# A four-layer graph network on one core: earlier rank prefix, eight term buffers, places in two pieces, and edge-row scatters moved between other work

## The chip, the cores and the metric

The kernel runs on 1 core of one Trainium2 chip, as one launch. The metric is device microseconds of one execution; lower is better. The time before is the median of 3 runs.

## The reference, cut to what matters

Four graph layers over 3125 nodes (256 features) and 50,000 edges sorted by target, each added to a residual. The first, with attention, is the one that the change touches, together with the sum of edge attributes that the second layer needs:

```python
def gat_conv(h, src, dst, W, al, ar, residual):
    feat = (h @ W).reshape(N, H, D)
    el = jnp.sum(feat * al, axis=-1)
    er = jnp.sum(feat * ar, axis=-1)
    e = jax.nn.leaky_relu(el[src] + er[dst], 0.2)
    ex = jnp.exp(e - emax[dst])
    a = ex / denom[dst]
    rst = jax.ops.segment_sum(feat[src] * a[:, :, None], dst, num_segments=N)
    ...
# layer 0: gat_conv twice.  Layer 1:
sum3d = segment_sum(edge_attr @ W_sum + b_sum, src, num_segments=num_nodes)
cent_term = sigmoid(centralities @ W_cent + b_cent)
vor_term = sigmoid(voronoi_values @ W_vor + b_vor)
```

Layer 2 sums by relation, layer 3 has two convolutions with batch norm.

## The kernel before, in words

The program has three phases (two attention passes, a middle, a tail). All that changes lies in the first. Edges are 392 columns of 128; nodes are 25 tiles of 128. The engines run hand-written streams that meet at semaphores.

**Setup.** PE makes 25 encoder products (L1218) for the cent and vor terms, ACT takes their sigmoids into `sigb` (L1152, three buffers in turn; a buffer is free again once its sum is stored), POOL adds the two halves (L1133, "the sums") and SP stores the result to `term_d` (L1099). DVE meanwhile ranks half of the edges by source tile (`rank_half`): a table (L577), a running sum along it (L580), totals per tile (L585), then a wait for three small products of PE (`rank_prefix`, L616 to L618, issued on PE behind encoder tile 8), and from these the places `attr_pos` to which the 196 edge columns of this half go (L599 to L611, one increment of `s_pos`). After that DVE makes the id columns, the low bits (L1197, turned by PE behind the encoder), the first norm, the second half's ranks, masks and step tables.

**Scatter.** Edge attributes must be added up by source, though the edges are sorted by target. SP loads seven columns at a time into one of three buffers `abuf` (`stage_attr`, L529 and L531), and POOL scatters each column to its sorted place in `attr_d` (L568). A buffer is loaded again when its seven scatters have landed. A half of the edges is 28 groups, 196 columns.

**A pass.** PE, ACT and DVE look up the attention scores of all edges (L866 to L969, 98 groups, "the look"), DVE takes a softmax by scans (L987 to L1023), ACT raises it and sends it to HBM and back (L1060 to L1065). Then come 220 steps: POOL gathers the feature rows of an edge pair into a ring of 28 slots (L179, two indirect DMAs a pair, 392 a pass), ACT scales them (L241, L246) and counts the pair ready, PE multiplies by one-hot matrices (L374) and DVE adds (L299). Beside each step runs one over the sorted attribute rows of that half, which SP loads from `attr_d` (`load_sorted_attr`, L258). A slot is gathered anew when the steps that use it are done: pair 28 waits for the first step (L239 counts the slot free).

**The order on POOL** is written out: 25 sums, 196 scatters of the first half, 392 gathers of pass one, 196 scatters of the second half, 392 gathers of pass two. SP's order follows it: three groups staged at the start, then the term stores, the low bits, the other groups of the half, three groups of the second half, the sorted rows.

Of the kernel before, what the change touches and what calls it, by code (L numbers as in the profile page):

```python
# [6 lines left out]
ALU = mybir.AluOpType  # L7
ACT = mybir.ActivationFunctionType
AX = mybir.AxisListType
# [43 lines left out]
GROUP = 7  # L53
GROUPS = HC // GROUP
BUFS = 3
LOOKS = EC // 4
# [23 lines left out]
def gnn_program(nc, t, out):  # L80
# [92 lines left out]

    def gather_pairs(pool, g, table, index, ring):
        for u in range(PAIRS):
# [229 lines left out]
    def carve(area, at, shape, dt=F32):  # L405
# [67 lines left out]
    carry = carve(arena_flat[0:HEADS, :], ARING * AW, (3, P))  # L473
    sigb = carve(arena_flat, ARING * AW, (3, 2 * D))
    term_rows = term_d.rearrange("(n p) f -> n p f", p=P)
# [18 lines left out]
        sem(x) for x in ("enc_zeroed", "enc_load", "encoded", "sigmoids", "terms_added"))  # L494
    term_stored = [sem(f"term_stored{k}") for k in range(3)]
    s_back = [sem(f"terms_back{k}") for k in range(5)]
    staged = [sem(f"staged{k}") for k in range(BUFS)]
# [43 lines left out]
    def load_terms(sp, q):  # L541
        k = q - TERM_FROM
        if k == 0:
            sp.wait_ge(s_exw, 32)
            for b in range(3):
                sp.wait_ge(term_stored[b], 16 * len(range(b, NT, 3)))
        if 0 <= k < 5:
            sp.dma_start(term[:, 5 * k:5 * k + 5, :],
                         term_d.rearrange("(n p) f -> p n f", p=P)[:, 5 * k:5 * k + 5, :]).then_inc(s_back[k], 16)

    def sp_weights(sp, l, first):
        for g in range(first, GROUPS):
            stage_attr(sp, GROUPS * l + g)
        if l == 0:
            for g in range(BUFS):
                stage_attr(sp, GROUPS + g)
        sp.wait_ge(s_sum[l], LOOKS + 2)
        for k in range(BUFS):
            sp.wait_ge(scattered[k], 16 * GROUP * len(range(k, GROUPS * (l + 1), BUFS)))
        load_sorted_attr(sp, steps[l], l, aring, between=(lambda q: load_terms(sp, q)) if l else None)  # L560

    def pool_scatter(pool, l):
        pool.wait_ge(s_pos, l + 1)
        for g in range(GROUPS * l, GROUPS * (l + 1)):
            at = GROUP * g
            pool.wait_ge(staged[g % BUFS], 32 * (g // BUFS + 1))
            for k in range(GROUP):
                pool.indirect_dma_start(  # L568
                    out=attr_d, in_=abuf[:, g % BUFS, k, :], in_offset=None,
                    out_offset=bass.IndirectOffsetOnAxis(ap=attr_pos[:, at + k:at + k + 1], axis=0),  # L570
                ).then_inc(scattered[g % BUFS], 16)

    def rank_half(dve, h):
# [23 lines left out]
        dve.drain()  # L597
        for n in range(NT):
            dve.scalar_tensor_tensor(out=running[:, n, :], in0=running[:, n, :], scalar=offset[:, n:n + 1],  # L599
                                     in1=mk[:, n, :], op0=ALU.add, op1=ALU.mult)  # L600
        dve.drain()
        dve.reduce_sum(pos[:, :], running.rearrange("p n j -> p j n"), AX.X)
        dve.drain()
        dve.tensor_copy(pos_i[:, 0, :], pos[:, :])
        dve.drain()
        dve.tensor_scalar(pos_i[:, 1, :], pos_i[:, 0, :], 7, None, ALU.logical_shift_right)
        dve.drain()
        dve.tensor_scalar(pos_i[:, 0, :], pos_i[:, 0, :], P - 1, None, ALU.bitwise_and)
        dve.tensor_scalar(pos[:, :], pos_i[:, 1, :], float(h * HC * P), None, ALU.add)
        dve.drain()  # L610
        dve.scalar_tensor_tensor(out=attr_pos[:, at:at + HC], in0=pos_i[:, 0, :], scalar=float(HC),  # L611
                                 in1=pos[:, :], op0=ALU.mult, op1=ALU.add).then_inc(s_pos, 1)

# [119 lines left out]
    def spread_tables(pe):  # L733
        pe.wait_ge(s_sp, 1)
        pe.matmul(p_last[0:NT, 0:PAIRS], ones[0:1, 0:NT], last_f[0:1, :], start=True, stop=True).then_inc(s_sp, 1)
        pe.wait_ge(s_prefix, 2)
        pe.wait_ge(s_pos, 2)
        pe.matmul(p_rank[0:NT, 128:130], upto[0:NT, 0:NT], col_f[0:NT, :], start=True, stop=True)\
# [132 lines left out]
    def act_look(act, l):  # L871
# [34 lines left out]
    def dve_look(dve, l):  # L906
# [4 lines left out]
        if l == 0:  # L911
            for k in range(3):
                dve.wait_ge(term_stored[k], 16 * len(range(k, NT, 3)))
        dve.tensor_copy(tab[:, 0, :], flat)
# [154 lines left out]
    with nc.Block() as block:  # L1069
        @block.sync  # L1070
        def _(sp):
# [25 lines left out]
            for n in range(NT):  # L1097
                sp.wait_ge(s_term, n + 1)
                sp.dma_start(term_rows[n, :, :], sigb[:, n % 3, 0:D]).then_inc(term_stored[n % 3], 16)  # L1099
            for q in range(2):  # L1100
                for c in range(4):
                    sp.wait_ge(s_loc, 4 * q + c + 1)
                    sp.dma_start(lo_d[q, c * QC:(c + 1) * QC, :], loT[0:QC, 4 * q + c, :]).then_inc(s_low, 16)
            sp_weights(sp, 0, BUFS)
            sp.wait_ge(steps[0].step_done, T + NHOT)
            sp.wait_ge(steps[0].attr_done, T + NHOT)
            sp_weights(sp, 1, BUFS)
            for k in range(3):
                sp.wait_ge(kept[k], 16 * (9 if k == 0 else 8))
            for k in range(5):  # L1110
                sp.wait_ge(s_back[k], 16)

        @block.gpsimd
        def _(pool):
# [16 lines left out]
            for n in range(NT):  # L1131
                pool.wait_ge(s_sig, n + 1)
                pool.tensor_tensor(sigb[:, n % 3, 0:D], sigb[:, n % 3, 0:D], sigb[:, n % 3, D:2 * D], ALU.add)\  # L1133
                    .then_inc(s_term, 1)
            pool.wait_ge(s_ready, 2)
            pool_scatter(pool, 0)
# [11 lines left out]
        def _(act):  # L1148
            for n in range(NT):
                act.wait_ge(s_enc, n + 1)  # L1150
                wait_from(act, term_stored[n % 3], 16 * (n // 3))
                act.activation(sigb[:, n % 3, :], banks[n % 2][:, :], ACT.Sigmoid).then_inc(s_sig, 1)  # L1152
            act_first_project(act)
# [834 lines left out]
```

## Time and profile before

| | before |
|---|---|
| runs, median | 3409.36 us (3409.08, 3409.36, 3410.53) |
| profiled execution | one such execution; its span, first to last instruction, is 3410.2 us |
| POOL busy | 2412.8 us (71%) |
| PE busy | 2202.9 us (65%), mean granted clock 0.833 |
| DVE busy | 2099.5 us (62%) |
| ACT busy | 1368.3 us (40%) |
| DMA | 465.58 MB, 137 GB/s |

The profiled execution's own time is not listed apart from the three; its span lies between the lowest and the highest of them. Busy shares are means over stages: the first attention pass ends near 875 us, the second near 1638 us, the middle and tail fill the rest. Of POOL's DMA instructions the busy time is that of making the descriptors; the data move afterwards.

### The profile page before, as it was taken

The numbers are of one execution on the slowest core, as the hardware profiler recorded it, in microseconds if no ns is written. First come the engines' busy times: TensorE is split into PE (matmuls) and PEld (weight loads), VectorE is DVE, ScalarE is ACT, GpSimd is POOL, SyncE is SP. The second block draws the span as 40 slices with busy tenths as digits, with TensorE's granted clock in tenths as the row PEclk, the third lists the DMA queues.
The fourth block names the chain that finished last, engine by engine and source line by source line (L and its number), as shares of the span: only waits on it lengthen the run. The fifth ranks groups of instructions, "written<-read, shape, count | busy, mean of one in ns | idle before, by whom it ended". The sixth has DMA issues, their size and how long they took to land. (4 is left out here: it accounts for less than half of the span.)

```text
span 3410.2 us, 73948 instructions
## 1 busy us (share of the span) xinstructions
PE 2202.9 (65%) x11271; PEld 1571.4 (46%) x11272; DVE 2099.5 (62%) x5434; ACT 1368.3 (40%) x4627; POOL 2412.8 (71%) x2428
## 2 busy tenths in 40 slices
PE   5566367776665377766786666675666675666666
PEld 2355355555455265555434444453444444444443
DVE  7999877666499867766774444454444444444445
ACT  2366389998566399988670000020000013000004
POOL 5877767777777777777737777757777753777772
PEclk9789789988899789988797777787777887777787
DMA  4488734443688654443783333423333322333331
GB/s 141 120 215 229 223 101 137 137 126 104 183 230 225 198 152 145 138 121 105 208 277 110 109 109 109 125 91 107 108 108 108 109 72 87 108 109 107 109 107 55
DMA packets 347323, 465.58 MB, mean 137 GB/s; under 512 B 112217, under 2 KB 262972, under 8 KB 343812
## 3 DMA queue, kind: packets, MB, share of 16 engines
q0 software_dynamic: 111808, 284.19, 28.9%
q1 hardware_dynamic: 161972, 111.43, 11.3%
q10 hardware_dynamic: 73236, 67.28, 7.3%
q14 instruction: 288, 2.36, 0.2%
q8 instruction: 19, 0.31, 0.0%
HBM read 385.51 MB, written 76.97 MB: 136 GB/s over the span
## 5 line engine op out<-in xcount | busy, mean ns | idle before, releaser
L374 PE MATMUL t_ps<-t_ring,shared 128*128 x2640 | 920.8, 504 | 533.7 <-ACTq L218 439.8
L374 PEld LDWEIGHTS t_ps<-t_ring,shared 128*128 128x128 f32 x2640 | 611.6, 248 | 842.7 <-issue 748.2
L179 POOL DMA_INDIRECT ring<-feat_d,srcC x784 | 780.1, 995 | 253.4 <-issue 210.6
L179 POOL DMA_INDIRECT t_ring<-feat_d,srcC x756 | 725.5, 960 | 275.2 <-issue 216.6
L246 ACT ACTIVATE ring<-ring,exC 128x64 f32<-128x64 f32 x3136 | 788.2, 335 | 0.0
L374 PE MATMUL bank<-ring,arena 128*128 x1408 | 438.7, 438 | 166.6 <-ACT ring L246 129.7
L299 DVE TENSOR_TENSOR acc<-acc,t_ps 128x256 f32 x440 | 185.3, 421 | 519.6 <-PE t_ps L374 518.6
L568 POOL DMA_INDIRECT attr_d<-abuf,attr_pos x392 | 407.1, 1038 | 119.5 <-issue 119.5
L179 POOL DMA_INDIRECT t_ring<-rel_d,relC x378 | 358.6, 949 | 162.7 <-issue 106.5
L283 DVE TENSOR_SCALAR shared<-lane,dlocT,weightT 128x128 f32<-128x128 f32 x1320 | 410.0, 362 | 54.8 <-PE t_ps L374 27.5
L1747 ACT COPY t_ring<-t_pt 128x512 f32<-128x512 f32 (+1 forms) x8 | 4.2, 526 | 971.1 <-PE t_pt L1722 971.1
L374 PEld LDWEIGHTS bank<-ring,arena 128*128 128x128 f32 x1408 | 267.5, 211 | 240.0 <-issue 210.8
L969 PE MATMUL wide<-arena 128*128 128x100 bf16 x4704 | 260.5, 216 | 172.8 <-ACT arena L888 150.9
L969 PEld LDWEIGHTS wide<-arena 128*128 128x128 bf16 x4704 | 235.9, 103 | 197.8 <-DVE arena L930 106.2
L299 DVE TENSOR_TENSOR X<-X,t_ps 128x256 f32 x220 | 92.5, 420 | 251.0 <-PE t_ps L374 250.2
L299 DVE TENSOR_TENSOR acc<-acc,bank 128x261 f32 x352 | 150.3, 427 | 153.1 <-PE bank L374 146.0
L277 DVE TENSOR_TENSOR arena<-lane,dlocT 128x256 f32<-128x256 f32 x440 | 185.1, 421 | 66.9 <-issue 32.1
L884 ACT ACTIVATE arena<-arena,minus_part 128x512 bf16<-128x512 bf16 x196 | 141.4, 721 | 180.3 <-issue 114.2
L936 DVE TENSOR_TENSOR arena<-wide,shared 128x800 f32<-128x800 f32 x196 | 191.3, 976 | 8.6 <-PE wide L969 8.0
L1688 ACT ACT_TABLE_LOAD x1 | 1.3, 1283 | 485.5 <-DVE mv L1675 485.5
L945 DVE TENSOR_REDUCE shared<-arena 128x800 f32 (+1 forms) x196 | 190.4, 972 | 0.1
L364 PEld LDWEIGHTS bank<-arena 128*128 128x128 f32 x704 | 142.7, 206 | 71.8 <-issue 45.8
(307 smaller groups left out, 2615.9 us busy)
## 6 DMA issues: line engine op xcount, KB each, us to landing
arena<-lo_d ACTq DMA_DIRECT2D x392, 128.0 KB
t_ring<-feat_d SPq DMA_DIRECT2D x1664, 1.0 KB
t_ring<-feat_d ACTq DMA_DIRECT2D x1664, 1.0 KB
rel_d<-mid_stage SPq DMA_DIRECT2D x25, 1024.0 KB, 4.6
arena<-attr_d SPq DMA_DIRECT2D x98, 260.0 KB, 3.1
abuf<-in_attr SPq DMA_DIRECT2D x56, 448.0 KB
t_ring<-rel_d SPq DMA_DIRECT2D x832, 1.0 KB
t_ring<-rel_d ACTq DMA_DIRECT2D x832, 1.0 KB
```

The costliest lines, as they stand in the source:

```text
L179: pool.indirect_dma_start(out=ring[:, u % RING, j, 0:D], out_offset=None, in_=table, in_offset=bass.IndirectOffsetOnAxis(ap=index[:, u, j: ...
L246: last = act.activation(part_of_row, part_of_row, ACT.Copy, scale=exC[:, bass.ds(u, 1), j, h])
L277: last = dve.tensor_tensor(hot[:, k % NHOT, :, :], lane[:, :].unsqueeze(1).to_broadcast([P, 2, P]), dlocT[:, bass.ds(s, 1), :].rearrange(" ...
L283: last = dve.tensor_scalar(hot[:, k % NHOT, j, :], lane[:, :], dlocT[:, bass.ds(s, 1), j], weightT[:, bass.ds(s, 1), j], ALU.is_equal, ALU ...
L299: dve.tensor_tensor(acc[:, tile, 0:g.width], acc[:, tile, 0:g.width], ps[k % NHOT][:, 0:g.width], ALU.add).then_inc(g.added, 1)
L364: pe.matmul(ps_a[k % NHOT][:, 0:AW - 1], hot_a[:, k % NHOT, :], aring[:, slot, 0:AW - 1], start=True, stop=True).then_inc(g.attr_done, 1)
L374: last = pe.matmul(ps[k % NHOT][:, 0:g.width], hot[:, k % NHOT, j, :], ring[:, slot, j, 0:g.width], start=(j == 0), stop=(j == 1))
L568: pool.indirect_dma_start(out=attr_d, in_=abuf[:, g % BUFS, k, :], in_offset=None, out_offset=bass.IndirectOffsetOnAxis(ap=attr_pos[:, at ...
L884: act.activation(apart[:, k % 2, :], lo[:, k, 1, :], ACT.Abs, bias=minus_part[:, 0:1])\
L936: dve.tensor_tensor(cand[:, k % 2, :, :, :], pk[k % 2][:, :, :].rearrange("p b (s x) -> p (b s) x", x=P)[:, :, 0:HEADS * NT] .rearrange("p ...
L945: dve.tensor_reduce(e[:, bass.ds(4 * c, 4), :], cand[:, k % 2, :, :, :].rearrange("p (j q) h n -> p j h q n", q=2), AX.XY, ALU.add).then_i ...
L969: last = pe.matmul(pk[k % 2][:, j // 2, at:at + HEADS * NT], looked[:, k % 2, q, j * P:(j + 1) * P], tab[:, piece, q * HEADS * NT:(q + 1) ...
```

## The change

1. `rank_prefix(pe, 0)` stands behind encoder tile 3 instead of tile 8.
2. `sigb` has eight buffers instead of three, at another place of the arena; everything that uses that place later waits for the term stores.
3. The places of the first half come in two pieces, columns 0 to 27 and 28 to 195, each with its own increment of `s_pos`.
4. From sum 12 on, POOL issues one scatter behind each sum: 13 of the first half's 196 stand between and right behind the sums.
5. 35 of the second half's scatters (five groups) stand behind the first 28 pairs' gathers of pass one; the other 161 stay behind the last gather of that pass.
6. SP stages groups 3 and 4 ahead of the low bits, and of the second half five groups ahead of the sorted rows of pass one and three more between them. With three buffers, groups 31 and 32 wait for scatters of groups 28 and 29.

```diff
+FIRST = 4 * GROUP
+EARLY = 5
+SIGS = 8
+MEET = 12
...
-    sigb = carve(arena_flat, ARING * AW, (3, 2 * D))
+    sigb = carve(arena_flat, 4624, (SIGS, 2 * D))
...
+    def stage_later(sp, q):
+        if 12 <= q < 12 + BUFS:
+            stage_attr(sp, GROUPS + EARLY + q - 12)
...
         if l == 0:
-            for g in range(BUFS):
+            for g in range(EARLY):
                 stage_attr(sp, GROUPS + g)
         sp.wait_ge(s_sum[l], LOOKS + 2)
...
-        load_sorted_attr(sp, steps[l], l, aring, between=(lambda q: load_terms(sp, q)) if l else None)
+        load_sorted_attr(sp, steps[l], l, aring, between=(lambda q: (load_terms if l else stage_later)(sp, q)))
...
+    def scatter_column(pool, c):
+        g, k = c // GROUP, c % GROUP
+        if c == 0 or c == FIRST or c == HC:
+            pool.wait_ge(s_pos, 1 + (c >= FIRST) + (c >= HC))
+        if k == 0:
             pool.wait_ge(staged[g % BUFS], 32 * (g // BUFS + 1))
...
+        for r in (slice(0, FIRST), slice(FIRST, HC)) if h == 0 else (slice(0, HC),):
+            place_columns(dve, h, r)
+
+    def place_columns(dve, h, r):
+        w = r.stop - r.start
+        if w == FIRST:
+            dve.tensor_tensor(running[:, :, r], running[:, :, r],
+                              offset[:, :].unsqueeze(2).to_broadcast([P, NT, w]), ALU.add)
+            dve.drain()
+            dve.tensor_tensor(running[:, :, r], running[:, :, r], mk[:, :, r], ALU.mult)
+        else:
+            for n in range(NT):
+                dve.scalar_tensor_tensor(out=running[:, n, r], in0=running[:, n, r], scalar=offset[:, n:n + 1],
+                                         in1=mk[:, n, r], op0=ALU.add, op1=ALU.mult)
...
-        pe.wait_ge(s_pos, 2)
+        pe.wait_ge(s_pos, 3)
...
             act.wait_ge(s_low, 16 * 8)
+            for k in range(SIGS):
+                act.wait_ge(term_stored[k], TERM_STORES[k])
...
+            for g in range(BUFS, BUFS + 2):
+                stage_attr(sp, g)
             for q in range(2):
                 for c in range(4):
                     sp.wait_ge(s_loc, 4 * q + c + 1)
...
-            sp_weights(sp, 0, BUFS)
+            sp_weights(sp, 0, BUFS + 2)
...
-            sp_weights(sp, 1, BUFS)
+            sp_weights(sp, 1, EARLY + BUFS)
...
+                if n == MEET:
+                    pool.wait_ge(s_ready, 2)
+                if n >= MEET:
+                    scatter_column(pool, n - MEET)
+            for c in range(NT - MEET, HC):
+                scatter_column(pool, c)
...
-            gather_pairs(pool, steps[0], feat_d, srcC, ring)
-            pool_scatter(pool, 1)
+            gather_pairs(pool, steps[0], feat_d, srcC, ring, range(0, RING))
+            for c in range(HC, HC + EARLY * GROUP):
+                scatter_column(pool, c)
+            gather_pairs(pool, steps[0], feat_d, srcC, ring, range(RING, PAIRS))
+            for c in range(HC + EARLY * GROUP, 2 * HC):
+                scatter_column(pool, c)
...
-                wait_from(act, term_stored[n % 3], 16 * (n // 3))
+                wait_from(act, term_stored[n % SIGS], 16 * (n // SIGS))
...
-                if n == 8:
+                if n == 3:
                     pe.wait_ge(s_ready, 1)
                     rank_prefix(pe, 0)
```

POOL, from the sums to the end of pass one's gathers. L568 is a scatter, L179 a gather, L1133 a sum; in the changed kernel they are L577, L183 and L1157. Before:

```order
L1133 TENSOR_TENSOR arena<-arena 128x256 x25
L568 DMA attr_d<-abuf,attr_pos 50176x130 x196
L1140 MEMSET ring 128x56
L179 DMA ring<-feat_d,srcC 128x256 x392
L568 DMA attr_d<-abuf,attr_pos 50176x130 x196
```

The same stretch of the changed kernel, from the last of the alternating sums on:

```order
L1157 TENSOR_TENSOR arena<-arena 128x256
L577 DMA attr_d<-abuf,attr_pos 50176x130 x184
L1168 MEMSET ring 128x56
L183 DMA ring<-feat_d,srcC 128x256 x56
L577 DMA attr_d<-abuf,attr_pos 50176x130 x35
L183 DMA ring<-feat_d,srcC 128x256 x336
L577 DMA attr_d<-abuf,attr_pos 50176x130 x161
```

Twelve scatters stand singly between the last thirteen sums, and 35 have moved from behind all 392 gathers to behind the first 56.

SP, where pass one's sorted rows are loaded (L258 before, L262 now; L529 and L531, now L534 and L536, stage a group). Before:

```order
L529 DMA abuf<-in_attr 128x7x128
L531 DMA abuf<-src_f 128x7x1
L258 DMA arena<-attr_d 128x520 x49
L529 DMA abuf<-in_attr 128x7x128
```

And in the changed kernel:

```order
L534 DMA abuf<-in_attr 128x7x128
L536 DMA abuf<-src_f 128x7x1
L262 DMA arena<-attr_d 128x520 x13
L534 DMA abuf<-in_attr 128x7x128
L536 DMA abuf<-src_f 128x7x1
L262 DMA arena<-attr_d 128x520
```

Two more pairs of staging stand ahead of the first load of sorted rows, and three stand between the loads, from the thirteenth on.

## Rows read from the trace of the kernel before

**Rows 1.** The page: busy us, share of the span and instructions of each engine.
```profile
PE 2202.9 (65%) x11271; PEld 1571.4 (46%) x11272; DVE 2099.5 (62%) x5434; ACT 1368.3 (40%) x4627; POOL 2412.8 (71%) x2428
```
**Rows 2.** POOL's groups: count, busy us, mean ns, idle before. Stretch 71 to 345.6.
```profile
L568 POOL DMA_INDIRECT attr_d<-abuf,attr_pos x196 | 215.0, 1097 | 59.6 <-issue 59.6
```
**Rows 3.** The same, stretches 345.6 to 424, then 438 to 868.3.
```profile
L179 POOL DMA_INDIRECT ring<-feat_d,srcC x56 | 60.6, 1081 | 16.9 <-issue 16.8
L179 POOL DMA_INDIRECT ring<-feat_d,srcC x336 | 327.8, 976 | 117.1 <-issue 86.9 <-ACTq L239 30.2
```
**Rows 4.** The same, stretches 868.3 to 1120.1, then 1120.1 to 1199.25.
```profile
L568 POOL DMA_INDIRECT attr_d<-abuf,attr_pos x196 | 192.0, 980 | 59.8 <-issue 59.8
L179 POOL DMA_INDIRECT ring<-feat_d,srcC x56 | 62.1, 1108 | 17.1 <-issue 17.1
```
**Rows 5.** POOL's timeline: start, us, instruction [idle before]. Gathers 56 and 57, pass one.
```profile
422.20 0.95 POOL L179 DMA_INDIRECT ring<-feat_d,srcC  x1 [0.30 <-issue]
438.15 0.95 POOL L179 DMA_INDIRECT ring<-feat_d,srcC  x1 [14.99 <-ACTq L239]
```
**Rows 6.** POOL's timeline: gather 57 of pass two.
```profile
1199.30 0.95 POOL L179 DMA_INDIRECT ring<-feat_d,srcC  x1 [0.31 <-issue]
```
**Rows 7.** PE's timeline: the first step of pass one and of pass two.
```profile
435.73 2.10 PE L374 MATMUL bank<-ring,arena 128*128 x4 [1.47 <-ACT ring L246]
1192.32 2.10 PE L374 MATMUL bank<-ring,arena 128*128 x4 [1.49 <-ACT ring L246]
```
**Rows 8.** ACT's groups in 438 to 600, then one of its groups in 438 to 870.
```profile
L246 ACT ACTIVATE ring<-ring,exC 128x64 f32<-128x64 f32 x616 | 154.8, 335 | 0.0
L241 ACT COPY ring<-exC 128x8 f32 x192 | 35.8, 187 | 39.2 <-issue 16.8 <-DMA ring<-feat_d,srcC 16.8 <-PE bank L374 5.4
```
**Rows 9.** POOL's timeline where the sums end and the scatters begin.
```profile
70.13 0.72 POOL L1133 TENSOR_TENSOR arena<-arena 128x256 f32<-128x256 f32 x1 [0.79 <-ACT arena L1152]
71.03 1.20 POOL L568 DMA_INDIRECT attr_d<-abuf,attr_pos  x1 [0.17 <-issue]
...
87.80 0.96 POOL L568 DMA_INDIRECT attr_d<-abuf,attr_pos  x1 [0.30 <-issue]
89.06 5.52 POOL L568 DMA_INDIRECT attr_d<-abuf,attr_pos  x1 [0.31 <-issue]
94.89 10.07 POOL L568 DMA_INDIRECT attr_d<-abuf,attr_pos  x1 [0.30 <-issue]
```
**Rows 10.** DVE's timeline: totals, the wait for the prefix, the second half's running sum.
```profile
23.75 0.61 DVE L585 TENSOR_TENSOR offset<-total,ring 128x25 f32<-128x25 f32 x1
41.86 0.15 DVE L587 COPY col_f<-wide 25x1 f32<-25x1 f32 x1 [17.50 <-PE wide L618]
...
93.82 10.37 DVE L580 TENSOR_TENSOR_SCAN ring<-ones,ring 128x4900 f32<-128x4900 f32 x1
```
**Rows 11.** PE's timeline: prefix, and the last encoder products.
```profile
40.59 0.62 PE L616 MATMUL wide<-total,before 128*128 128x25 f32 x2
...
57.27 12.14 PE L1218 MATMUL bank<-shared 4*128 4x512 f32 x14
```
**Rows 12.** ACT's timeline: sigmoids of tiles 3 and 4, 9 and 10.
```profile
32.83 1.08 ACT L1152 ACTIVATE arena<-bank 128x512 f32<-128x512 f32 x2 [19.89 <-DMA term_d<-arena]
...
43.85 0.60 ACT L1152 ACTIVATE arena<-bank 128x512 f32<-128x512 f32 x1 [2.56 <-PE bank L1218]
45.56 0.60 ACT L1152 ACTIVATE arena<-bank 128x512 f32<-128x512 f32 x1 [1.11 <-PE bank L1218]
```
**Rows 13.** Busy us of PE, PEld, DVE, ACT, POOL in two stretches; PEclk, DMA share, GB/s.
```profile
16.00:33.00 17.00, 0.00 (x0) 0.00 (x0) 8.21 (x4) 0.17 (x1) 8.30 (x2) 1.00 0.99 293
33.00:41.00 8.00, 7.53 (x10) 2.83 (x11) 0.00 (x0) 3.00 (x6) 3.57 (x5) 1.00 0.19 66
```
**Rows 14.** SP's timeline: loads of sorted rows. Waits in 875 to 1192: total, times, longest.
```profile
387.75 27.46 SPq L258 DMA_DIRECT2D arena<-attr_d  x16
PE bank L1053 <- DMA acc<-weight_d: 17.2, 1, 17.2
```

More of the change, by code:

```diff
@@ L172, in __init__, with gather_pairs @@
                 self.landed.append(at.at)
-    def gather_pairs(pool, g, table, index, ring):
-        for u in range(PAIRS):
+    def gather_pairs(pool, g, table, index, ring, pairs=range(PAIRS)):
+        for u in pairs:
             if u >= RING:
@@ L494, in gnn_program @@
         sem(x) for x in ("enc_zeroed", "enc_load", "encoded", "sigmoids", "terms_added"))
-    term_stored = [sem(f"term_stored{k}") for k in range(3)]
-    s_back = [sem(f"terms_back{k}") for k in range(5)]
+    term_stored = [sem(f"term_stored{k}") for k in range(SIGS)]
+    s_back = term_stored[0:5]
+    TERM_STORES = [16 * len(range(k, NT, SIGS)) for k in range(SIGS)]
     staged = [sem(f"staged{k}") for k in range(BUFS)]
@@ L544, in load_terms @@
             sp.wait_ge(s_exw, 32)
-            for b in range(3):
-                sp.wait_ge(term_stored[b], 16 * len(range(b, NT, 3)))
+            for b in range(SIGS):
+                sp.wait_ge(term_stored[b], TERM_STORES[b])
         if 0 <= k < 5:
@@ L559, in sp_weights @@
             sp.wait_ge(scattered[k], 16 * GROUP * len(range(k, GROUPS * (l + 1), BUFS)))
-        load_sorted_attr(sp, steps[l], l, aring, between=(lambda q: load_terms(sp, q)) if l else None)
[L562 to L565, printed above, removed]
-            pool.wait_ge(staged[g % BUFS], 32 * (g // BUFS + 1))
[L567 to L571, printed above, removed]
+        load_sorted_attr(sp, steps[l], l, aring, between=(lambda q: (load_terms if l else stage_later)(sp, q)))
[4 more added lines that the diff above has]
+        if k == 0:
+            pool.wait_ge(staged[g % BUFS], 32 * (g // BUFS + 1))
+        pool.indirect_dma_start(
+            out=attr_d, in_=abuf[:, g % BUFS, k, :], in_offset=None,
+            out_offset=bass.IndirectOffsetOnAxis(ap=attr_pos[:, c:c + 1], axis=0),
+        ).then_inc(scattered[g % BUFS], 16)
     def rank_half(dve, h):
@@ L597, in rank_half @@
         dve.drain()
-        for n in range(NT):
-            dve.scalar_tensor_tensor(out=running[:, n, :], in0=running[:, n, :], scalar=offset[:, n:n + 1],
-                                     in1=mk[:, n, :], op0=ALU.add, op1=ALU.mult)
+        for r in (slice(0, FIRST), slice(FIRST, HC)) if h == 0 else (slice(0, HC),):
[11 more added lines that the diff above has]
+                                         in1=mk[:, n, r], op0=ALU.add, op1=ALU.mult)
         dve.drain()
-        dve.reduce_sum(pos[:, :], running.rearrange("p n j -> p j n"), AX.X)
+        dve.reduce_sum(pos[:, r], running[:, :, r].rearrange("p n j -> p j n"), AX.X)
         dve.drain()
-        dve.tensor_copy(pos_i[:, 0, :], pos[:, :])
+        dve.tensor_copy(pos_i[:, 0, r], pos[:, r])
         dve.drain()
-        dve.tensor_scalar(pos_i[:, 1, :], pos_i[:, 0, :], 7, None, ALU.logical_shift_right)
+        dve.tensor_scalar(pos_i[:, 1, r], pos_i[:, 0, r], 7, None, ALU.logical_shift_right)
         dve.drain()
-        dve.tensor_scalar(pos_i[:, 0, :], pos_i[:, 0, :], P - 1, None, ALU.bitwise_and)
-        dve.tensor_scalar(pos[:, :], pos_i[:, 1, :], float(h * HC * P), None, ALU.add)
+        dve.tensor_scalar(pos_i[:, 0, r], pos_i[:, 0, r], P - 1, None, ALU.bitwise_and)
+        dve.tensor_scalar(pos[:, r], pos_i[:, 1, r], float(h * HC * P), None, ALU.add)
         dve.drain()
-        dve.scalar_tensor_tensor(out=attr_pos[:, at:at + HC], in0=pos_i[:, 0, :], scalar=float(HC),
-                                 in1=pos[:, :], op0=ALU.mult, op1=ALU.add).then_inc(s_pos, 1)
+        dve.scalar_tensor_tensor(out=attr_pos[:, h * HC + r.start:h * HC + r.stop], in0=pos_i[:, 0, r],
+                                 scalar=float(HC), in1=pos[:, r], op0=ALU.mult, op1=ALU.add).then_inc(s_pos, 1)
     def rank_prefix(pe, h):
@@ L911, in dve_look @@
         if l == 0:
-            for k in range(3):
-                dve.wait_ge(term_stored[k], 16 * len(range(k, NT, 3)))
+            for k in range(SIGS):
+                dve.wait_ge(term_stored[k], TERM_STORES[k])
         dve.tensor_copy(tab[:, 0, :], flat)
@@ L1098, in _ @@
                 sp.wait_ge(s_term, n + 1)
-                sp.dma_start(term_rows[n, :, :], sigb[:, n % 3, 0:D]).then_inc(term_stored[n % 3], 16)
+                sp.dma_start(term_rows[n, :, :], sigb[:, n % SIGS, 0:D]).then_inc(term_stored[n % SIGS], 16)
+            for g in range(BUFS, BUFS + 2):
+                stage_attr(sp, g)
             for q in range(2):
@@ L1110, in _ @@
             for k in range(5):
-                sp.wait_ge(s_back[k], 16)
+                sp.wait_ge(s_back[k], TERM_STORES[k] + 16)
         @block.gpsimd
@@ L1132, in _ @@
                 pool.wait_ge(s_sig, n + 1)
[L1133 to L1136, printed above, removed]
+                pool.tensor_tensor(sigb[:, n % SIGS, 0:D], sigb[:, n % SIGS, 0:D], sigb[:, n % SIGS, D:2 * D],
+                                   ALU.add).then_inc(s_term, 1)
+                if n == MEET:
[4 more added lines that the diff above has]
+                scatter_column(pool, c)
             for k in range(5):
@@ L1150, in _ @@
                 act.wait_ge(s_enc, n + 1)
-                wait_from(act, term_stored[n % 3], 16 * (n // 3))
-                act.activation(sigb[:, n % 3, :], banks[n % 2][:, :], ACT.Sigmoid).then_inc(s_sig, 1)
+                wait_from(act, term_stored[n % SIGS], 16 * (n // SIGS))
+                act.activation(sigb[:, n % SIGS, :], banks[n % 2][:, :], ACT.Sigmoid).then_inc(s_sig, 1)
             act_first_project(act)
```

## The prediction

> **What bounds the kernel now.** I read the busy time of each engine first [rows 1]: POOL is the busiest, with 71% of the span, and all that it does in the first phase are indirect DMAs. So the next view was POOL's groups by stretch [rows 2 to 4]. Adding busy time and the idle time just before, 196 scatters of the first half take 274.6 us, 56 gathers 77.5, 336 gathers 430 (1.28 each, its one long wait left out), 196 scatters of the second half 251.8 (1.285 each) and 56 gathers of pass two 79.2. In these the idle time is 0.3 us per instruction, the gap between two DMA instructions of one engine: POOL runs without a pause. In the whole stretch from 71 us on it stands still at one place for long: after 56 gathers of pass one, from 423.15 to 438.15, 15.0 us [rows 5], because the ring of 28 pairs is full and the first step is not done. That step ends at 435.73 + 2.10 = 437.83 [rows 7], and POOL goes on 0.32 later. In pass two nothing of the kind shows: the first step ends at 1192.32 + 2.10 = 1194.42, so the slot for pair 28 is free near 1194.7, but POOL comes to gather 57 only at 1199.30 [rows 6, 7]. There POOL is late by 4.6 us.
>
> From the full ring on, who sets the end of a pass? The other side is ACT, the busiest of the consumers: in 438 to 600 it scaled 616/8 = 77 pairs in 162 us, 2.10 us a pair; POOL needs 2 x 1.28 = 2.56. ACT therefore eats up the lead of 28 pairs and then waits for gathers to land, 16.8 us in all [rows 8]. 196 pairs at 2.10 are 412 us; from the first scaling near 433 that would be 845, and the pass ends at 875. So POOL sets the end of both passes, with some 28 us between it and the next bound.
>
> From this follows the rule of the whole estimate. Time that POOL gains before the full ring is worth something only until the first step is done; time that it gains between the passes is worth 4.6 us and no more; time that it loses after the first step of pass one is paid in full.
>
> **The change part by part.**
>
> *Prefix behind tile 3 and eight buffers.* DVE's totals are ready at 24.36 and it waits 17.50 us for the prefix [rows 10], because PE has it behind tile 8, and the tiles stand still while ACT waits 19.89 us for a buffer that comes free with its store [rows 12]. With eight buffers and the product at tile 3, PE is idle when the totals come. The prefix takes 41.86 - 40.59 = 1.27 [rows 10, 11]: it is done at 25.6, 16 us earlier. ACT's sigmoid after a prefix came 2.0 later, the following ones every 1.71 [rows 12]: tile 4 at 27.6, tile 12 at 41.3, tile 24 at 61.8 instead of 69.5. DVE's next wait is then for the encoder's last product: PE finished at 57.27 + 12.14 = 69.41 [rows 11], now near 61.5. DVE's chain through norm, tables, look and softmax comes out about 8 us earlier, not 16.
>
> The Trainium skill speaks against this edit (TensorE: Matmul & The Clock Gate, Part 1): an idle PE falls to half its clock and has to warm up. The rows say otherwise here: after 17 us without a product the next tiles ran at the usual 1.71, with a granted clock of 1.00 in both stretches [rows 12, 13]. I go by the rows. By the page, each encoder tile that ran at the lower level would cost another 1.7 us, and all that follows on POOL with it.
>
> *Places in two pieces.* DVE's places for the first 28 columns are ready some 6 us after the prefix, about 32; the first scatter cannot come before the sum of tile 12, near 42. This wait costs nothing, with 10 us to spare.
>
> *Scatters between the sums.* A sum takes 0.72 and 0.17 to the next DMA; a scatter 1.20 behind a sum, 0.96 behind its like, and 0.30 of gap [rows 9]. An alternating pair is 2.15 to 2.39, I take 2.3, so POOL and not ACT's 1.71 sets the pace. From 41.9 twelve pairs bring the last sum to 69.5, column 12 starts at 70.4, column 13 at 71.7; before, column 13 started at 87.80 [rows 9]. **Gain 16.1 us**; 14.5 with the dear scatter, 18 with the cheap. At ACT's pace it would be 22, its upper bound.
>
> *The rest of the first half and the ring.* The same instructions follow. Some of them were held by DVE's long operations (10.07 instead of 0.97 beside the running sum that ends at 104.19 [rows 9, 10]); DVE is 8 us earlier as well, so I keep these losses. The ring is full at 423.15 - 16.1 = 407.0.
>
> *35 scatters behind the full ring.* At 1.285 [rows 4]: 45.0 us. POOL resumes its gathers at 407.0 + 45.0 = **452.0 instead of 438.15: 13.9 us later**. The 15.0 us of waiting and the 16.1 gained are both spent, and 13.9 more. To be free the number would have had to be about 22 or less.
>
> *SP.* It now stages two more groups before the sorted rows, and these wait for the scatters of groups 28 and 29, done near 416 and 425; the first load went out at 387.75 before [rows 14]. The steps begin near 431 to 435, as before, so the 8 us that DVE gained are lost here. It costs nothing as long as the first step ends before 452. The three stagings between the loads wait until about 454; by then 14 loads, 56 columns, are in, and some 11 steps are done. Groups 3 and 4 ahead of the low bits move these by about 4 us; the look reads them 40 us later.
>
> *Pass one from there.* 336 gathers, 430 us, unchanged: the pass ends 13.9 later. The ring's lead is smaller, which changes nothing where POOL sets the end.
>
> *Pass two.* 161 scatters instead of 196 bring POOL to the full ring 45.0 us earlier against the end of pass one, but the first step's end hangs on DVE's chain, which starts with the end of pass one. POOL gains the **4.6 us** by which it was late and then waits 40 us. PE's wait of 17.2 for the weights' way to HBM and back [rows 14] may shrink when POOL is silent; between 0 and 3 us, I take **1**.
>
> **Sum:** +13.9 - 4.6 - 1.0 = **+8.3 us**. The times are from the profiled execution, span 3410.2, 0.8 above the median; the differences carry over. 3409.4 + 8.3 = **3417.7 us**. What this kernel's measurement can tell from no change is about 0.2%, 6.8 us.
>
> **The rivals.**
>
> *A: less than forecast, within 0.2%.* If the alternation ran at ACT's pace (gain 22) the sum would be +2.4; if, besides, the ring's gathers ran before DVE's scans and were not held (56 gathers took 77.5 us instead of 56 x 1.26 = 70.4 [rows 3]), -4.7. For it: the gap behind a sum was only 0.17. Against: POOL is in the ring's gathers until 407, and DVE, which moves by 8 us only, is in its softmax scans inside the same stretch. The Trainium skill (SBUF — State Buffer, section SBUF: two separate sides) has it that a DVE operation that takes the ports shared with GpSimd keeps them to its end, so that a POOL DMA waits for its descriptors; by that rule the trace agrees, with one scatter that ends 0.8 us after the running sum [rows 9, 10]. Time about 3412. Chance 0.25.
>
> *B: the ring's lead covers the late resume; faster.* If ACT, PE and DVE set the end of pass one, POOL's 13.9 us would vanish in the lead of 28 pairs, and what is left is the start of the steps, 1 to 8 us earlier, and the 4.6 of pass two with the 1 of the weights: -7 to -14, 3399. It decides if the consumers need more than 430/168 = 2.56 us a pair. Against it stand the 2.10 that they took and the 16.8 us that ACT waited for landings [rows 8]. Chance 0.08.
>
> *C: much slower.* If each change between sum and scatter cost a full microsecond more, or the encoder ran at the lower clock, the 16.1 would shrink to about 4: +20, 3430. The 1.20 of the first scatter [rows 9] speaks for 0.2, not 1. Chance 0.08.
>
> *D: the change doesn't do what it says*, because POOL waits for groups 3 or 4, staged only behind the last term store near 71: column 21 follows some 10 us after it. A late staging would stop POOL for a few us, +12, 3421. It lies within the range and counts with the forecast.
>
> **How the numbers follow.** The forecast, over +6.8, has 0.59; A 0.25; B 0.08; C 0.08. The terms' bounds (gain 14.5 to 18, scatters 44.5 to 45.5, weights 0 to 3) give +3.9 to +10.4 around 3417.7, and D 3421. To hold eight in ten the range goes down to A's time, rounded to 3410, and up to 3424, half way to C. Faster by over 0.2%: B, with a little of A, 0.09. Within 0.2%: 0.26. Slower: forecast and C, 0.65.
>
> **What would show it.** Right: DVE waits for the prefix 1 to 2 us instead of 17.5; column 13 starts near 72; POOL's waiting of 15.0 before gather 57 of pass one is gone, 35 scatters of about 45 us stand there and gather 57 starts near 452; the first load of sorted rows comes near 427; pass one's gathers end near 882; in pass two POOL waits about 40 us before gather 57, which starts near 1208. Wrong: gather 57 of pass one before 440, or the gathers behind it taking less than 430 us, or pass one ending less than 10 us after 875.

## The result, and the profile after

The changed kernel takes 3418.84 us, median of 7 runs (3413.25 to 3423.82), against 3409.36 before (3407.22 to 3411.67, 7 runs): a ratio of 1.0027, 95% interval 1.0016 to 1.0038, or 9.5 us more. The profiled execution is the median one, with a span of 3417.0 and a granted clock of 0.826.

The busy times, as in [rows 1]:

```profile
PE 2214.5 (65%) x11271; PEld 1578.0 (46%) x11272; DVE 2103.1 (62%) x5442; ACT 1369.9 (40%) x4627; POOL 2406.9 (70%) x2428
```

The engines do the same work as before, but for eight instructions and 3.6 us on DVE, so the shares tell nothing. What moved is seen in the timelines. PE's and DVE's, where the prefix is waited for:

```profile
24.98 0.60 PE L636 MATMUL wide<-total,before 128*128 128x25 f32 x2 [11.05 <-DVE offset L594]
26.11 36.20 PE L1250 MATMUL bank<-shared 4*128 4x512 f32 x42
26.21 0.14 DVE L596 COPY col_f<-wide 25x1 f32<-25x1 f32 x1 [1.39 <-PE wide L638]
62.73 0.51 DVE L1229 CAST ring<-wide 98x128 bf16<-98x128 f32 x2 [1.89 <-PE wide L1259]
```

DVE waits 1.39 for the prefix, not 17.50 [rows 10]; now PE waits 11.05 for DVE instead. The encoder ends at 62.31, not 69.41 [rows 11]. POOL's timeline, sums and scatters in turn, and the last of them:

```profile
42.54 0.73 POOL L1157 TENSOR_TENSOR arena<-arena 128x256 f32<-128x256 f32 x1 [0.98 <-ACT arena L1184]
43.44 1.20 POOL L577 DMA_INDIRECT attr_d<-abuf,attr_pos  x1 [0.17 <-issue]
44.67 0.74 POOL L1157 TENSOR_TENSOR arena<-arena 128x256 f32<-128x256 f32 x1
45.58 0.99 POOL L577 DMA_INDIRECT attr_d<-abuf,attr_pos  x1 [0.17 <-issue]
46.60 0.74 POOL L1157 TENSOR_TENSOR arena<-arena 128x256 f32<-128x256 f32 x1
...
67.32 0.98 POOL L577 DMA_INDIRECT attr_d<-abuf,attr_pos  x1 [0.17 <-issue]
68.61 0.97 POOL L577 DMA_INDIRECT attr_d<-abuf,attr_pos  x1 [0.30 <-issue]
```

A pair of sum and scatter takes 46.60 - 44.67 = 1.93 us; column 13 starts at 68.61 in place of 87.80 [rows 9], 19.2 earlier. POOL's timeline at the full ring, which answers to [rows 5]:

```profile
401.90 2.56 POOL L183 DMA_INDIRECT ring<-feat_d,srcC  x1 [0.30 <-issue]
...
448.53 0.97 POOL L577 DMA_INDIRECT attr_d<-abuf,attr_pos  x1 [0.30 <-issue]
449.80 0.98 POOL L183 DMA_INDIRECT ring<-feat_d,srcC  x1 [0.31 <-issue]
...
877.74 0.95 POOL L183 DMA_INDIRECT ring<-feat_d,srcC  x1 [0.30 <-issue]
...
1204.62 0.95 POOL L183 DMA_INDIRECT ring<-feat_d,srcC  x1 [47.87 <-ACTq L243]
```

The ring is full at 401.90 + 2.56 = 404.46, 18.7 earlier than the 423.15 of before. Then 35 scatters take 45.0 us and gather 57 starts at 449.80: 11.65 later than before. The last gather of pass one is 10.7 later than the 867.07 of before. In pass two POOL waits 47.87 us, and gather 57 is only 5.3 later than before [rows 6]. It waits so long partly because the 56 gathers ahead of it took 70.5 us, the longest 1.07, where before they took 78.8 and the longest 2.55.

The ends of both passes, before and after, are marked by two rows of DVE, the copy of `in_deg` behind the last step of pass one and the first operation on it behind pass two:

```profile
875.60 0.18 DVE L840 COPY in_deg<-acc 128x25 f32<-128x25 f32 x1
1641.17 1.78 DVE L1468 TENSOR_SCALAR mid_deg_f<-in_deg 128x25 f32<-128x25 f32 x1 [1.96 <-PEq L103]
```
```profile
886.78 0.17 DVE L860 COPY in_deg<-acc 128x25 f32<-128x25 f32 x1
1646.88 1.78 DVE L1500 TENSOR_SCALAR mid_deg_f<-in_deg 128x25 f32<-128x25 f32 x1 [2.28 <-PEq L107]
```

The changed kernel is 11.2 us behind at the first mark and 5.7 at the second. Behind the second mark no run changes the code; yet this stretch took between 1764.9 and 1770.6 us in the ten profiled executions outside the disturbed chip. Differences of a few us between two times or two spans can come from there, and the second mark is then the better measure.

SP and DVE before the first step:

```profile
423.67 0.38 SPq L534 DMA_DIRECT2D abuf<-in_attr  x1
424.09 0.62 SPq L536 DMA_DIRECT2D abuf<-src_f  x1
424.90 21.67 SPq L262 DMA_DIRECT2D arena<-attr_d  x13
429.44 0.55 DVE L295 TENSOR_SCALAR arena<-lane,arena,minus_tile 128x128 f32<-128x128 f32 x1 [9.21 <-SPq L266]
```

The staging of group 32 waits for its buffer until 423.67, the first load of sorted rows goes out behind it, and DVE waits 9.21 for the rows. Whether this wait costs anything is for the experiments.

### The profile page after: what moved, and what is told of

Its sections match the earlier page's. It is cut to its first block and busy times, and to the rows that moved or that the text cites. A ratio compares the mean times of both kernels' runs of the same rounds, so it can differ in the third digit from the quotient of the medians.

```text
span 3417.0 us, 73967 instructions
## 1 busy us (share of the span) xinstructions
PE 2214.5 (65%) x11271; PEld 1578.0 (46%) x11272; DVE 2103.1 (62%) x5442; ACT 1369.9 (40%) x4627; POOL 2406.9 (70%) x2428
## 3 DMA queue, kind: packets, MB, share of 16 engines
q1 hardware_dynamic: 161972, 111.43, 11.3%
## 5 line engine op out<-in xcount | busy, mean ns | idle before, releaser
L183 POOL DMA_INDIRECT ring<-feat_d,srcC x784 | 771.8, 984 | 286.3 <-issue 214.6
L183 POOL DMA_INDIRECT t_ring<-feat_d,srcC x756 | 725.5, 960 | 275.4 <-issue 214.7
L378 PE MATMUL bank<-ring,arena 128*128 x1408 | 446.5, 444 | 165.8 <-ACT ring L250 132.9
L577 POOL DMA_INDIRECT attr_d<-abuf,attr_pos x392 | 408.4, 1042 | 117.7 <-issue 117.7
L183 POOL DMA_INDIRECT t_ring<-rel_d,relC x378 | 358.6, 949 | 163.5 <-issue 107.0
```

The lines of the kernel that those rows point to most:

```text
L183: pool.indirect_dma_start(out=ring[:, u % RING, j, 0:D], out_offset=None, in_=table, in_offset=bass.IndirectOffsetOnAxis(ap=index[:, u, j: ...
L378: last = pe.matmul(ps[k % NHOT][:, 0:g.width], hot[:, k % NHOT, j, :], ring[:, slot, j, 0:g.width], start=(j == 0), stop=(j == 1))
L577: pool.indirect_dma_start(out=attr_d, in_=abuf[:, g % BUFS, k, :], in_offset=None, out_offset=bass.IndirectOffsetOnAxis(ap=attr_pos[:, c:c ...
```

## The experiments

All but the four runs named below as disturbed stand beside the kernel before at 3409.28. "Gather 57" is the first gather behind the full ring. "Set-up edits" are all parts of the change but the 35 scatters; of these the interleaving (experiment 5) and the place of the prefix (7 and 8) were tried by themselves, the eight buffers, the places in two pieces and the early groups 3 and 4 were not.

**1. The 35 scatters taken away again** (the set-up edits alone; three groups staged ahead of the sorted rows):

```
-EARLY = 5
+EARLY = 0
-            for g in range(EARLY):
+            for g in range(BUFS):
                 stage_attr(sp, GROUPS + g)
-        if 12 <= q < 12 + BUFS:
-            stage_attr(sp, GROUPS + EARLY + q - 12)
+        if 12 <= q < 12 + EARLY:
+            stage_attr(sp, GROUPS + BUFS + q - 12)
```

> The changed kernel with none of the second half's scatters behind the full ring (EARLY 0; three groups staged ahead of the sorted rows, as before). Theory (POOL's time before the full ring counts only until the first step is done, and the 35 scatters cost what they run past it): the ring is full near 404.5 as in the changed kernel, POOL waits some 24 us and resumes when the first step ends, near 429 because DVE's chain is 8 to 9 us earlier; 8.5 us off the 438.15 of before, pass two as before with POOL 5 us late: 3409.4 - 8.5 = 3401, between 3399 and 3403. Rival 1 (the set-up edits are worth nothing, the steps begin where they did): 3409. Rival 2 (POOL's 18.7 us count in full): 3391.

Measured: 3395.51 (ratio 0.9966, interval 0.9954 to 0.9979), 13.8 under before, 5.5 under my number and outside its range. Rivals 1 and 2 both fall: the edits are worth something, but not the 18.7 of POOL. Its POOL timeline, and DVE's before the first step:

```profile
424.98 0.95 POOL L183 DMA_INDIRECT ring<-feat_d,srcC  x1 [22.56 <-ACTq L243]
402.66 1.79 DVE L1045 TENSOR_TENSOR shared<-shared,acc 128x1568 f32<-128x1568 f32 x1
415.14 2.53 DVE L1054 COPY exC<-bank 128x392 f32<-128x392 f32 x4 [2.74 <-PE bank L1075]
```

The same two rows of DVE in the kernel before:

```profile
411.74 1.79 DVE L1023 TENSOR_TENSOR shared<-shared,acc 128x1568 f32<-128x1568 f32 x1
428.30 2.53 DVE L1032 COPY exC<-bank 128x392 f32<-128x392 f32 x4 [6.82 <-PE bank L1053]
```

The first step is done 13.2 earlier, not 8.5. 9.1 of it is DVE's chain (411.74 to 402.66); the other 4.1 come out of the weights' way to HBM and back. PE waits for it, in 400 to 440, before, here, and in the changed kernel:

```profile
PE bank L1053 <- DMA acc<-weight_d: 19.8, 1, 19.8
```
```profile
PE bank L1075 <- DMA acc<-weight_d: 15.7, 1, 15.7
```
```profile
PE bank L1075 <- DMA acc<-weight_d: 16.9, 1, 16.9
```

Before, POOL's gathers were still being issued beside it, up to 423.15; here POOL is silent from 402.4 on; in the changed kernel scatters stand there. That POOL's DMAs make the way longer is what these rows suggest. Experiment 5 bears it out: there, without the 35 scatters, gathers stand beside the way to its end, and PE waits 18.0 for it, not 15.7.

**2. Fourteen scatters behind the full ring** (as experiment 1, with `EARLY = 2`).

> 14 scatters behind the full ring in place of 35 (EARLY 2; three groups staged ahead of the sorted rows, two between their loads). Theory: 14 x 1.285 = 18.0 end near 422.5, inside the idle time, so gather 57 of pass one still starts near 429 and nothing is paid; pass two gains POOL's 5 us of being late and about 1 of the weights' round trip: 3401 - 6 = 3395, between 3393 and 3398. Rival 1 (the scatters disturb the start of the steps or the sorted rows' loads, so that they cost even inside the wait): 3401 or more. Rival 2 (pass two gains nothing): 3401.

Measured: 3393.77 (0.9956, 0.9943 to 0.9969). POOL:

```profile
420.87 1.27 POOL L577 DMA_INDIRECT attr_d<-abuf,attr_pos  x1 [0.30 <-issue]
425.18 0.98 POOL L183 DMA_INDIRECT ring<-feat_d,srcC  x1 [3.04 <-ACTq L243]
...
1180.58 0.95 POOL L183 DMA_INDIRECT ring<-feat_d,srcC  x1 [15.46 <-ACTq L243]
```

The 14 end at 422.1, gather 57 starts 0.2 later than without them: the scatters are free here, and rival 1 falls. In pass two POOL is no longer late; its gather 57 comes at 1180.58 against 1183.55 in experiment 1. These 3 us stand in the trace, but the two times' intervals overlap, so that the gain of pass two isn't resolved in the times. The absolute number fits (rival 2's 3401 lies outside the interval), but only because experiment 1 came out lower too: the step between the two, 1.7, is far from the 6 that I had. From here to the changed kernel 21 more scatters put gather 57 24.6 later and cost 25.1 in time.

**3. Forty-nine scatters** (`EARLY = 7`, nothing else).

> 49 scatters behind the full ring in place of 35 (EARLY 7). Theory (POOL sets the end of pass one): 14 x 1.285 = 18.0 more, gather 57 near 467.8, pass two unchanged since POOL already waits there for 48 us: 3418.8 + 18.0 = 3436.8, between 3435 and 3439. Rival (the lead of the ring and the consumers' pace cover part of a late resume): less than 10 more, 3419 to 3429.

Measured: 3432.28 (1.0069, 1.0056 to 1.0082), 13.4 over the changed kernel, outside both ranges, between the theory's 18 and the rival's 10.

```profile
467.95 0.98 POOL L183 DMA_INDIRECT ring<-feat_d,srcC  x1 [0.30 <-issue]
...
894.48 0.95 POOL L183 DMA_INDIRECT ring<-feat_d,srcC  x1 [0.30 <-issue]
```

Gather 57 is 18.15 later, as said, and the last gather 16.7: the 336 gathers take 426.5 in place of 427.9. From pass one's end to gather 57 of pass two another 2 us are gone (315.8 from DVE's copy of `in_deg` at 902.58, against 317.8). Why these stretches are shorter I haven't found; the rival's cover by the ring's lead isn't it for the gathers, since POOL waits for no slot there. Behind pass two it stands 16.05 later (1662.93 against 1646.88), and the rest of the difference from the measured 13.4 lies behind that mark, in the stretch that varies by itself. So POOL's time is paid at 9 parts in 10 by the traces, and at three quarters in the time.

**4. The 35 scatters alone, in the kernel before.** Its `gather_pairs` is split and five groups are scattered between:

```
-            gather_pairs(pool, steps[0], feat_d, srcC, ring)
-            pool_scatter(pool, 1)
+            gather_pairs(pool, steps[0], feat_d, srcC, ring, range(0, RING))
+            pool_scatter(pool, 1, 0, EARLY)
+            gather_pairs(pool, steps[0], feat_d, srcC, ring, range(RING, PAIRS))
+            pool_scatter(pool, 1, EARLY, GROUPS)
```

> The kernel before with the 35 scatters behind the full ring alone and nothing of the set-up edits. Theory: the ring is full at 423.15 as before, gather 57 of pass one at 423.2 + 45.0 = 468.2 in place of 438.15, +30.0; pass two gains 5 for POOL being late and 1 for the weights: 3409.4 + 30 - 6 = 3433, between 3431 and 3437, so the set-up edits are worth 14 to 18 in the changed kernel. Rival (the set-up edits' gain on POOL doesn't reach the end): within 3 of the changed kernel, 3416 to 3422.

Measured: 3437.61 (1.0089, 1.0076 to 1.0102), at the upper edge of my range and a little over it. Gather 57:

```profile
470.42 0.98 POOL L180 DMA_INDIRECT ring<-feat_d,srcC  x1 [0.31 <-issue]
```

2.2 later than expected, since its ring was full at 425.10, 2 us later than in the profile of before. The rival's 3416 to 3422 falls. With experiment 1 this gives all four corners: 3409.3 with neither part, 3395.5 with the set-up edits, 3437.6 with the scatters, 3418.8 with both. The scatters cost 28.3 in the old set-up and 23.3 in the new; the set-up edits are worth 13.8 without them and 18.8 with them.

**5. No interleaving of sums and scatters**, with 35 scatters and with none:

```
-                if n == MEET:
-                    pool.wait_ge(s_ready, 2)
-                if n >= MEET:
-                    scatter_column(pool, n - MEET)
-            for c in range(NT - MEET, HC):
+            pool.wait_ge(s_ready, 2)
+            for c in range(HC):
                 scatter_column(pool, c)
```

These two, experiment 6 and experiment 7 ran first on a chip on which the kernel before, too, took 4859.56 us:

> The changed kernel, 35 scatters kept, with all 25 sums ahead of the first scatter again. Theory (POOL is without a pause from the first scatter to the end of pass one): the sums run at ACT's pace of 1.71, the last ends near 63.3, column 13 near 63.5 + 13 x 1.27 = 80.0 in place of 68.6, and these 11.4 us are paid in full: 3418.8 + 11.4 = 3430.2, between 3428 and 3433. Rival (the interleaving only moves work that DVE's long operations hold up anyway): under 5 more.

> As the run above without interleaving, but with no scatter behind the full ring (EARLY 0). Theory (POOL's gain before the full ring counts only until the first step is done): the ring is full near 416 and the first step is done near 424.7 as with EARLY 0 and interleaving, so the interleaving is worth nothing here: 3395.5, between 3393 and 3398. Rival: the 11.4 us appear here too, 3407.

Measured: 4855.50 and 4857.37 (0.9999, 0.998 to 1.0017, and 1.0007, 0.9993 to 1.0021). Nothing can be read from these times. DVE there stands waiting inside the look, as this row of the waits in 100 to 540 of experiment 7's kernel shows (total, times, longest); the changed kernel's profile has no wait for "remote" in that stretch:

```profile
DVE arena L958 <- remote: 287.4, 5, 65.2
```

What held that chip up is open. In the first 70 us the same kernels agree with their second run within a microsecond. Both ran again elsewhere:

> The kernel with the 35 scatters and no interleaving once more, on a chip that is not held by its DMAs. Its own trace has column 13 at 80.7 in place of 68.6, 12.1 later. Theory (POOL's time is paid in full with 35 scatters): 3418.8 + 12.1 = 3430.9, between 3428 and 3434. Rival: DVE's long operations swallow part of it, under 5 more than the changed kernel.

> No interleaving and no scatter behind the full ring, once more. Theory: the ring is full near 417, the first step is done near 424.7, or up to 2 later because more of the weights' way to HBM and back stands beside gathers; POOL waits some 8 us: 3395.5 to 3398. Rival (the interleaving is worth its 12.1 us here too): 3407.

Measured: 3430.10 (1.0054, 1.004 to 1.0068) and 3398.84 (0.9964, 0.9951 to 0.9978). With 35 scatters, the first scatter, column 12 and gather 57; then gather 57 with none:

```profile
63.45 1.20 POOL L577 DMA_INDIRECT attr_d<-abuf,attr_pos  x1 [0.17 <-issue]
...
79.67 5.83 POOL L577 DMA_INDIRECT attr_d<-abuf,attr_pos  x1 [0.30 <-issue]
...
461.39 0.98 POOL L183 DMA_INDIRECT ring<-feat_d,srcC  x1 [0.30 <-issue]
```
```profile
425.89 0.95 POOL L183 DMA_INDIRECT ring<-feat_d,srcC  x1 [9.42 <-ACTq L243]
```

Column 12 starts 12.3 later than the 67.32 of the changed kernel; it then takes 5.83 beside a long operation of DVE, and column 13 takes 10.07. In the changed kernel two scatters are held likewise, columns 22 and 23 (5.84 and 10.07). So the hold is not what differs. The edit costs 11.6 us at gather 57 and 11.3 in time where POOL has no slack, and 0.9 and 3.3 where it waits anyway. The 3.3 isn't resolved (that ratio's interval holds experiment 1's 0.9966), though it puts the time 0.8 over my range; the rival's 3407 falls. This is the rule of the estimate, shown both ways.

**6. SP not held by groups 31 and 32**: experiment 1's staging, with `EARLY = 5`, so that three groups are staged ahead of the sorted rows and five between their loads.

> The changed kernel, 35 scatters kept, but SP stages only three groups of the second half ahead of the sorted rows and the other five between their loads, so that the first load goes out near 378 in place of 424.9. Theory: the steps begin near 420 in place of 429.4, but POOL resumes its gathers at 449.8 all the same and sets the end: 3418.8, between 3416 and 3421. Rival (the late start of the steps, 9.2 us of waiting on DVE for sorted rows, costs part of itself): 3410 to 3415.

4831.60 on the disturbed chip (0.9948, 0.9932 to 0.9965), and again:

> The changed kernel with 35 scatters and SP not held by groups 31 and 32, once more. Theory: the first load of sorted rows near 378, the steps from 420 in place of 429.4, gather 57 at 449.8 all the same: 3418.8, between 3416 and 3421. Rival: 3410 to 3415.

Measured: 3416.01 (1.0018, 1.0009 to 1.0027; the changed kernel 1.0027, 1.0016 to 1.0038). SP, DVE and POOL:

```profile
377.79 20.59 SPq L262 DMA_DIRECT2D arena<-attr_d  x13
420.12 0.35 DVE L295 TENSOR_SCALAR arena<-lane,arena,minus_tile 128x128 f32<-128x128 f32 x1
450.40 0.98 POOL L183 DMA_INDIRECT ring<-feat_d,srcC  x1 [0.30 <-ACTq L243]
```

DVE's wait of 9.21 is gone and the steps begin 9.3 earlier, but gather 57 starts no earlier (450.40 against 449.80), and DVE's copy behind the last step comes at 887.13 against 886.78. The wait cost nothing at the end of the pass, nor behind pass two, where this kernel stands at 1647.39 against 1646.88. Its time is 2.8 us lower, at the lower edge of my range, with intervals that overlap; this difference arises behind both passes, in the stretch that varies by itself.

**7. The prefix behind tile 8 again.** The row of PE with 11.05 us of waiting suggested that tiles 4 to 8 could run there:

```
-                if n == 3:
+                if n == 8:
                     pe.wait_ge(s_ready, 1)
                     rank_prefix(pe, 0)
```

> The changed kernel with the prefix products behind encoder tile 8 again (as before), eight buffers and all else kept. The trace of the changed kernel shows PE idle for 11.05 us between tile 3 and the prefix, since DVE's totals come at 24.8. Theory: tiles 4 to 8 run in this gap, the prefix still comes at 25, and tiles 9 and on come 5 x 1.71 = 8.5 us earlier; sum 12 ends near 34.8, column 13 starts near 60, the ring is full near 396, gather 57 starts near 441.3, all of it paid or gained in full: 3418.8 - 8.5 = 3410.3, between 3408 and 3413. Rival 1 (with the eight buffers the encoder is held by the term stores, or the prefix comes later than 25 as in the kernel before): no gain, 3417 to 3422. Rival 2 (POOL's time is hidden behind DVE's holds): half the gain, 3414.

It ran on the disturbed chip (4848.98; 0.9978, 0.9959 to 0.9996), so that its time says nothing; its column 13 came at 66.49. The same prefix and buffers are in the next experiment, and its rows show how much is to be had.

**8. The best of both**: experiment 2 with the prefix behind tile 8.

> 14 scatters behind the full ring and the prefix behind encoder tile 8. With eight buffers ACT then waits at tile 8 for the first term store, until 33.4, so POOL gains 2.1 us, and the encoder ends at 60.0 in place of 62.3, DVE's casts begin 1.4 earlier. Theory (DVE's chain sets the first step when 14 scatters stand there): 1.4 off the run with 14 scatters, 3392.4, between 3390 and 3394. Rival (POOL's time decides): 2.1 off, 3391.7, not to be told apart from it; or no gain: 3394.

Its early rows, of PE, ACT, SP and POOL:

```profile
24.50 0.59 PE L636 MATMUL wide<-total,before 128*128 128x25 f32 x2 [1.77 <-DVE offset L594]
32.37 1.08 ACT L1184 ACTIVATE arena<-bank 128x512 f32<-128x512 f32 x2 [10.71 <-DMA term_d<-arena]
25.33 37.34 SPq L1121 DMA_DIRECT2D term_d<-arena  x24
65.69 0.97 POOL L577 DMA_INDIRECT attr_d<-abuf,attr_pos  x1 [0.30 <-issue]
```

Tiles 4 to 8 do run in the gap: PE now waits 1.77 there, not 11.05, and the prefix comes no later than the 24.98 of the changed kernel. But then all eight buffers are full, and ACT waits until 32.37 for the first term store, which SP issues only at 25.33, behind its setup loads. Rival 1 of experiment 7 has it in the main: column 13 comes 2.9 us earlier than in the changed kernel, not 8.5. The same stop, at tile 3 of the kernel before, is the 19.89 of [rows 12]. So with eight buffers the prefix needs no earlier place; its place only decides where the encoder stands still. Three buffers with the prefix at tile 3 weren't tried.

Measured: 3391.98 (0.9948, 0.9935 to 0.9962), 17.3 under before and the fastest of all. DVE's copy of the weights starts at 413.24 (415.15 in experiment 2), gather 57 at 423.35 (425.18), still behind 4.13 us of waiting, and the last gather of pass one at 850.15 against 853.51. So DVE's chain, not POOL, set the first step here, as the theory had it. The order of the two kernels is in the traces; their times' intervals overlap.

## Why the prediction was right

**The rule.** POOL's time before the full ring counts only until the first step is done, and is paid afterwards: shown by experiments 5 (11.3 against nothing that can be told apart), 2 (14 scatters free, the next 21 paid with 25.1 for 24.6) and 1 (the ring is full 20.7 earlier than before, POOL resumes 13.2 earlier, as the first step does). "In full" is not shown for every case: in experiment 3 it was paid at 13.4 for 18.

**Interleaving: right in kind, mis-sized.** I took 2.3 us a pair; it was (67.32 - 43.44) / 12 = 1.99, and 1.92 in the undisturbed pairs. The term that failed is the gap: I had 0.30 in front of the sum, as between two DMAs; the sum starts 0.03 behind the scatter. Column 13 gained 19.2, not 16.1, above my bound of 18, and gather 57 was 11.65 late, not 13.9. Rival A argued from the other gap, the 0.17 behind a sum, which I had in my sum already; the gain lies halfway between my 16.1 and its 22.

**35 scatters, 45.0 us:** 45.04.

**SP and the steps:** the load came at 424.9 (I had 427) and the steps began at 430 (I had 431 to 435); no cost at the end of the pass (experiment 6).

**336 gathers, 430:** 427.9 from start to start of the first and the last, against 428.9 before in the same count. By its letter this is one of the signs that I had named for being wrong (under 430 us); but the kernel before meets it too, so the sign was set badly and says nothing.

**Pass two, -4.6 and -1:** between the ends of the passes' steps and gather 57 the changed kernel gained 11.18 - 5.32 = 5.9. The weights' way took 15.8 in place of 17.2 [rows 14]; that is 1.4 where I took 1, and the 4.6 by which POOL was late make up the rest. POOL waited 47.87 where I had 40, since its 56 gathers ran 8.3 faster than before. That they would not be held was the second term of rival A; it came true in pass two, where it is worth nothing, and not in pass one (77.4 us, before 77.3).

**The sum.** At the end of pass two the changed kernel stands at +5.7, where I had +8.3, and 1.1 more are in the span. The medians differ by 9.5. The other 2.7 I put down to the execution of before, which is an inference and not shown: its span alone is 0.8 above the median, while in each profiled run here the time is 1.7 to 2.8 above the span, so that this execution was probably 2.5 us or more above the median. I had set its span against the median. That 3417.7 came so near 3418.8 is luck: a sum that was 2.6 too high at the end of pass two, and 3.8 us that it didn't contain (1.1 behind the passes, 2.7 from the choice of the execution). The mechanism held, the nearness is no measure of it.

**What I missed outside the sum.** The way to HBM and back counts in pass one as well: 19.8 in the kernel before, 15.7 in experiment 1. I costed it in pass two alone. In the changed kernel it is hidden behind the scatters; in experiment 1 it made 4.1 of the 5.5 by which my number was too high. I also called about 22 scatters free; the wait that experiment 1 left open, 22.56 us, holds 17 at 1.285. And I gave the prefix's new place a part in the gain that it doesn't have beside eight buffers (experiment 8).

**Slips in the working.** With the bounds that I named the sum reaches +11.4, not +10.4 (45.5 - 15.0 - 14.5 - 4.6), 3420.8 and still within the range. At ACT's pace of 1.71 column 13 would gain about 23, not 22, and 56 x 1.26 is 70.6, not 70.4. None of them moves the forecast.

**The rivals.** A falls as a whole: its 3412 lies below the interval, which begins at 1.0016. Whether the loss exceeds 0.2% is not settled, since the median does and that end of the interval doesn't. B falls: the kernel is slower, not faster, a later gather 57 is paid (experiments 2 and 3), and with the steps 9 us earlier the end of the pass stays (experiment 6). C falls, the pair was cheaper and the clock in 40 to 100 was 1.00. D did not occur: POOL's scatters of groups 3 and 4 follow without a wait.

## What to carry to other kernels

An engine that works off its instructions in order and sets the end has slack only where it waits: measure that wait in the changed program, not in the old one, and fill it to its size. Here 14 of the moved scatters were free and the other 21 cost 25 us, while a gain of that engine made ahead of such a wait bought nothing that could be resolved until something filled it (experiment 5). When buffers are added because one engine waits for a store, look for what stands ahead of the first store on the queue that issues it.

## What the hardware showed that I had not expected

- On POOL an elementwise sum behind an indirect DMA starts 0.03 us after it and a DMA behind a sum 0.17, where two indirect DMAs have 0.30 between them: a pair takes 1.92, less than 0.30 + 0.73 + 0.17 + 0.98.
- PE's wait for the weights' round trip through HBM differed with what POOL issued beside it: 17.2 to 19.8 us beside ring gathers (before in both passes, and pass two of experiment 1), 16.4 to 17.0 beside scatters, 15.7 to 15.9 with POOL silent. The 4.1 of experiment 1 compares the highest of these with the lowest; why the gathers of before cost 19.8 in pass one and 17.2 in pass two is open.
- One chip took 4860 us for a kernel that takes 3409 on the others, with the same times, within a microsecond, in the first 70 us.
